# History loads in three pieces, turns in the order of landing, and a uniform step on TensorE

## The reference

```
q = (target_item @ W_q).reshape(b, H, HD)
k = (history_sequence @ W_k).reshape(b, S, H, HD)
v = (history_sequence @ W_v).reshape(b, S, H, HD)
scores = jnp.einsum('bhd,bshd->bhs', q, k) / SCALE
scores = jnp.where(mask[:, None, :] == 0, NEG, scores)
attn = jax.nn.softmax(scores, axis=-1)
out = jnp.einsum('bhs,bshd->bhd', attn, v).reshape(b, A)
return out @ W_o
```

## Time and profile before

| | before |
|---|---|
| median of 3 runs | 578.87 us (578.73 to 581.99) |
| the profiled execution: time, span | 578.07 us, 576.1 us |
| PE, DVE busy | 538.1 us (93%), 504.2 us (88%) |
| ACT, POOL busy | 291.3 us (51%), 309.2 us (54%) |
| HBM | 217.58 MB read, 380 GB/s over the span |
| chain that ended last | PE 71%, DVE 17%, DMA 5%, issue 5% |
| DVE turns (L475) | 320, 472.1 us busy |

### The profile page before, as it was taken

One profiled execution on the slowest core, in us unless ns is written; L12 is line 12 of the kernel. 1 busy time (PEld: TensorE's weight loads), 2 busy tenths in 40 slices (PEclk: granted clock), 3 DMA queues, 4 the chain that ended last, 5 costly groups with the idle time before them and its releaser, 6 DMA issues.

```text
span 576.1 us, 41624 instructions
## 1 busy us (share of the span) xinstructions
PE 538.1 (93%) x18604; PEld 437.8 (76%) x18604; DVE 504.2 (88%) x577; ACT 291.3 (51%) x949; POOL 309.2 (54%) x1126
## 2 busy tenths in 40 slices
PE   5597999999999999999999899999999999999996
PEld 4475878778787877877787787878778787877875
DVE  5657899999999899999998999999999999999970
ACT  2053545554555555455555545545554554555453
POOL 6653456465655556565555556556465645646500
PEclk9799999999999999999999999999999999999999
DMA  8967999999999999999999999999999999999950
GB/s 327 416 259 278 354 406 411 402 405 405 412 404 409 405 406 405 405 413 398 410 406 403 385 395 408 406 403 409 405 405 405 409 402 399 410 407 401 402 213 7
DMA packets 47687, 219.04 MB, mean 380 GB/s; under 512 B 5696, under 2 KB 14416, under 8 KB 47648
## 3 DMA queue, kind: packets, MB, share of 16 engines
q1 hardware_dynamic: 46368, 217.35, 94.8%
q0 software_dynamic: 704, 1.05, 0.5%
q10 hardware_dynamic: 576, 0.25, 0.2%
HBM read 217.58 MB, written 1.05 MB: 380 GB/s over the span
## 4 chain that ended last, share of the span: by engine, by line
PE 71%; DVE 17%; DMA 5%; issue 5%; SPq 1%; ACT 0%; DVEq 0%; POOLq 0%; POOL 0%
PE ps_s L251 27%; PE ps_c L281 23%; DVE blocks L475 15%; PE ps_p L264 7%; PE ps_y L291 6%; PE ps_u L239 3%; PE ps_u L298 3%; DMA x_t<-r_target_item 3%; DMA hist<-r_history_sequence 2%; DVE probs_t L496 1%; SPq L153 1%; PE ps_y L306 1%; ACT p_pad L410 0%; DVE inv_sum L491 0%; SPq L144 0%
## 5 line engine op out<-in xcount | busy, mean ns | idle before, releaser
L475 DVE STREAM_TRANSPOSE blocks<-hist 128x768 f32<-128x768 f32 (+2 forms) x320 | 472.1, 1494 | 25.4 <-DMA hist<-r_history_sequence 23.2
L199 POOL COPY u_pad<-u_sb 32x32 f32<-32x32 f32 x1024 | 236.3, 231 | 111.6 <-ACT u_sb L389 53.7
L251 PE MATMUL ps_s<-blocks,u_pad 128*32 128x200 f32 x4096 | 193.7, 335 | 16.5 <-DVE blocks L475 14.4
L281 PE MATMUL ps_c<-hist,p_pad 64*32 64x128 f32 x12800 | 199.8, 271 | 4.0 <-issue 3.1
L281 PEld LDWEIGHTS ps_c<-hist,p_pad 64*32 64x32 f32 x12800 | 181.8, 105 | 19.8 <-issue 17.3
L410 ACT ACTIVATE p_pad<-ps_p,own 128x200 f32<-128x200 f32 x512 | 170.1, 443 | 42.4 <-PE ps_p L264 42.4
L251 PEld LDWEIGHTS ps_s<-blocks,u_pad 128*32 128x32 f32 x4096 | 122.8, 109 | 72.2 <-issue 26.5
L203 POOL TENSOR_SCALAR bias<-mask 128x200 f32<-128x200 int32 x64 | 56.5, 883 | 128.1 <-DMA mask<-r_mask 127.7
L419 ACT COPY ctx_sb<-ps_c 128x128 f32<-128x128 f32 x128 | 27.8, 269 | 88.5 <-PE ps_c L281 88.5
L393 ACT ACTIVATE probs<-neg_score,neg_max 128x200 f32<-128x200 f32 x64 | 29.4, 459 | 81.2 <-DVE neg_max L484 81.1
L264 PE MATMUL ps_p<-probs_t,place_sel 128*64 128x112 f32 x1024 | 63.7, 267 | 0.8 <-DVE probs_t L496 0.5
(11 more groups left out here) (42 smaller groups left out, 93.0 us busy)
## 6 DMA issues: line engine op xcount, KB each, us to landing
hist<-r_history_sequence SPq DMA_DIRECT2D x128, 832.0 KB, 8.6
hist<-r_history_sequence SPq DMA_DIRECT2D x128, 768.0 KB, 5.9
mask<-r_mask SPq DMA_DIRECT2D x64, 100.0 KB, 8.6
out<-out_sb POOLq DMA_DIRECT2D x21, 48.0 KB, 5.3
x_t<-r_target_item SPq DMA_DIRECT2D x1, 976.0 KB, 16.1
w_in<-L_rec_W_k ACTq DMA_DIRECT2D x1, 64.0 KB, 2.0
w_in<-L_rec_W_q SPq DMA_DIRECT2D x1, 64.0 KB, 2.2
w_in<-L_rec_W_v ACTq DMA_DIRECT2D x1, 64.0 KB, 6.7
```

The lines of the kernel that those rows point to most:

```text
L199: pool.tensor_copy(to, source[Q * c:Q * c + Q, a]).then_inc(u_pad_ready, 1)
L251: mm = pe.matmul(ps_s[ring][Q * b:Q * b + Q, 0:S].rearrange("p (t j) -> p t j", j=J), u_pad[ring][:, i, b, c, :], blocks[slot][:, :, c, J ...
L281: mm = pe.matmul(ps_c[alpha][at:at + Q, 0:D], p_pad[rows, t + par, i, :], hist[2 * ring + i][rows, t + par, :], start=(t == 0), stop=(t + ...
L475: dve.transpose(blocks[g % BLOCKS][:, t0:t1].rearrange("p t c k -> p (t c k)"), hist[g % SLOTS][:, t0:t1, :].rearrange("p t d -> p (t d)") ...
```

## The change

The history of a group is loaded in three pieces of 6, 9 and 10 columns, each with its own semaphore and its own release by the context. DVE turns each piece by itself, six turns a pair, in the order in which they are loaded. PE's step is the same for all three steps of a round: place, turn_context, both scores, context; the projection or the outputs stand between the second and the third piece of the context. The projection of a round is made two rounds ahead, half of the heads in the second step and half in the third; those of rounds 0 and 1 are made before the loop. The target rows of the first two rounds are loaded early on ACT's queue, the rest behind the history of pair 2, and the wait for them moves into the projection. The wait for the expanded weights moves to the last matmul of the scores. ACT copies the projection and the outputs ahead of the context. Cut to its core:

```
-    HALVES = ((0, 12), (12, T))
+    PIECES = ((0, 6), (6, 15), (15, T))
+    SIGNAL = (0, 1, 2)
...
             for p in range(NP):
-                for h, (t0, t1) in enumerate(HALVES):
+                for h, (t0, t1) in enumerate(PIECES):
                     for i in range(2):
                         g = 2 * p + i
-                        wait(sp, ctx_done, 2 * (p - RING) + h + 1)
+                        wait(sp, ctx_done, len(PIECES) * (p - RING) + h + 1)
...
-                if p == 1:
-                    sp.dma_start(x_t[:, ROUND:B], target_t[:, ROUND:B]).then_inc(rest_loaded, 16)
+                if p == 2:
+                    sp.dma_start(x_t[:, 2 * ROUND:B], target_t[:, 2 * ROUND:B]).then_inc(rest_loaded, 16)
...
-            def combine(r):
+            def combine(r, heads):
                 if not isinstance(r, int):
-                    pe.wait_ge(u_copied, r)
+                    pe.wait_ge(rest_loaded, 16)
+                    if heads[0] == 0:
+                        pe.wait_ge(u_copied, r)
                 at = r * ROUND
-                for h in range(H):
+                for h in heads:
...
+                        if released is not None and c == 3 and b == B4 - 1:
+                            pe.wait_ge(expanded, released)
...
                 place(q)
-                if ring < 2:
-                    pe.wait_ge(ctx_copied, 2 * q + 2)
-                    turn_context()
-                    if ring == 0:
-                        combine(r + 1)
-                    if ring == 1:
-                        outputs(q - 1)
-                    scores(q + 1, after, 0)
-                    pe.wait_ge(expanded, q + 1)
-                    scores(q + 1, after, 1)
+                pe.wait_ge(ctx_copied, 2 * q + 2)
+                turn_context()
+                scores(q + 1, after, 0)
+                scores(q + 1, after, 1, q + 1)
+                for piece in range(len(PIECES) - 1):
+                    context(ring, piece)
+                if ring == 0:
+                    outputs(q)
                 else:
-                    scores(q + 1, after, 0)
-                    scores(q + 1, after, 1)
-                    pe.wait_ge(expanded, q + 1)
-                    pe.wait_ge(ctx_copied, 2 * q + 2)
-                    turn_context()
-                context(ring, 0)
-                context(ring, 1)
+                    combine(r + 2, (2 * ring - 2, 2 * ring - 1))
+                context(ring, len(PIECES) - 1)
...
+            pe.wait_ge(u_copied, 1)
+            combine(1, range(H))
             warm(WARM[0])
             scores(0, 0, 0)
             scores(0, 0, 1)
-            pe.wait_ge(rest_loaded, 16)
             warm(WARM[1])
...
-            act.dma_start(x_t[:, 0:ROUND], target_t[:, 0:ROUND]).then_inc(x_loaded, 16)
+            act.dma_start(x_t[:, 0:2 * ROUND], target_t[:, 0:2 * ROUND]).then_inc(x_loaded, 16)
...
                 normalise(q)
+                r = q // RING
+                if q % RING == 0 and r + 1 < NR:
+                    copy_combined(r + 1)
+                if q % RING == 1 and r >= 1:
+                    store(r - 1)
                 if q >= 1:
                     finish(q - 1)
...
                 if p < NP:
-                    turn(p, 1, 0, 0, 6)
+                    turn(p, 1, 0)
                 if p >= 1:
                     reciprocal(p - 1)
                 if p < NP:
-                    turn(p, 1, 0, 6, 12)
+                    turn(p, 0, 1)
                 if p >= 1:
                     turn_probs(p - 1)
                 if p < NP:
-                    turn(p, 0, 1)
                     turn(p, 1, 1)
+                    turn(p, 0, 2)
+                    turn(p, 1, 2)
```

## The result

The changed kernel takes 592.77 us (median of 4 runs, 590.92 to 593.22), the kernel before 580.43 us beside it: a ratio of 1.0225, interval 1.0188 to 1.0262. It is 12 us slower; 581.5 us was forecast, and the range ended at 588.

A forecast was written before the change was run, and what follows sets the result against it. Transfers, PE and DVE were all taken to stand within a few per cent of the step, tied by chains. First maximum +1.0, 63 steps +2.2, tail +0.2: +3.4 us on 578.07 gives 581.5 us, range 577 to 588.

The forecast's parts named there:

- The six turns in the order of landing: DVE, 44 columns behind the maximum for 38: a floor of 8.63 us a step, 0.26 us over 8.37.
- The chain of 8.63 us runs from the first M on: Loop start, M being the maximum's start: target rows in two parts end the slow start, gaining 14.1 us.
- The projection of round 1 before the loop: Ahead of the first warm-up: eight more matmuls delay the first maximum by 1.0 us, bounds 0.8 to 2.0.
- PE's order: PE's step with the projection inside the context: 8.63 us in a round's first step, 8.19 us in the others.
- The wait for the expanded weights: Before the last score matmul: ACT's eight copies, 2.66 us, end before the wait, covered by the scores.
- ACT's order: ACT's projection and output copies ahead of the context's: 0.6 us beside place and turn, hidden.
- The pieces: Six history transfers a pair for four: loss at joints 0.35 us for 0.23, hidden; DMA share under 1.
- the transfers bound it and the early release pays: Rival, 8%: DMA sets the step, 551 us at 8.14 us a step, 565 us with only the start repaired.
- the two equal chains add up: Rival, 20%: in a round's first step PE's and DVE's 8.63 us have no slack between them; together 589 us.

The follow-up runs named there:

- eights: The changed kernel with pieces of 8, 8 and 9 columns instead of 6, 9 and 10: 587.52 us, ratio to the kernel before 1.011.
- split_only: The kernel before with only the turn of 12 columns cut into 6 ahead of the maximum and 6 behind: 599.94 us, ratio 1.0331.
- two_ahead: The changed kernel with both turns of 6 columns ahead of the maximum: 577.91 us, ratio to the kernel before 0.9962.
- start_only: The kernel before with only the target rows of two rounds loaded early, the rest behind pair 2: 577.63 us, ratio 0.9972.
- warm_more: The changed kernel with 28 transposes instead of 16 ahead of the loop: 593.16 us.
- sixes: The changed kernel with both turns of 6 ahead of the maximum, projection and outputs outside the context, pieces 6, 6, 13: 575.86 us.
- peel: The changed kernel with the first round of three steps written out ahead of the loop: 922.82 us, ratio 1.5943.

## Why the prediction missed, point by point

**The six turns in the order of landing: right, with luck in the last 0.04 us.** 8.63 us from maximum to maximum forecast, 8.64 measured in all three steps. The chain that was added up ends with the pair's last turn and the second half of the scores. In the trace the last turn ends at 313.11, and 313.11 + 1.68 would be 8.60 us from maximum to maximum. The scores, though, run as one group of 64 behind one wait, that for the last turn of group 0 (it ends at 311.72, the scores start at 311.85 and take 2.98 us to the maximum: 8.64). In the step with the outputs PE does not wait at all, and its own order of 8.63 us is the limit. The prediction had left out the second way, which eights shows as the longer one; that it came out equal here is chance. split_only shows that the turns alone do it, two_ahead that without them the loss is gone. The slope was read right (1.28 us for a turn of 9). The floor as such is shown.

**"The chain of 8.63 us runs from the first M on": wrong, by 10.2 us.** This is the step that failed. I had taken the slow start of 14.1 us as one thing that goes away with the wait for the target rows. It was three. The wait for the rows put the first place 6 us late (27.24 us, against 21.21 in start_only); that wait did go away, and the place started at 22.33 us where 22 was forecast. PE's pauses for its code, 5.2 us, stood in the same stretch and stayed (6.35 us after). So did a stretch at half the clock. Before, it made the 16 transposes take 3.65 us and the first place 1.53, after 1.97 and 0.99; after, it cost 1.7 us in the first step (warm_more) and 1.5 us behind the longest pause (1.10 for 0.61 and 2.30 for 1.30). Pauses and half clock are together 9.5 of the 10.1 us that four steps lose against steady ones. start_only measures the term by itself: the first four steps get 4.7 us shorter, the fifth maximum comes 4.0 us earlier and the medians differ by 2 us, where 13 were counted on. With the 46.7 us of before kept for these four steps, the prediction's sum gives a span of 591.7 us; 591.3 were measured. The rows that showed it lay in front of me: the chain of the kernel before lists the pauses as "issue" at 35, 45 and 51 us, and I had read only the waits that had a name.

**The projection of round 1 before the loop: right in kind, 1.5 us for 1.0.** The warm-up started 1.82 us behind it, PE had begun 0.68 us later (11.34 us against 10.66), and the shorter warm-up (3.25 us against 4.29) gave 1.04 back.

**PE's order: right.** The step with the outputs was read as 8.63 us and measured as 8.65 in two_ahead, where nothing else covers it. The Trainium skill ("TensorEngine Tiling (Array Packing)", Key Properties) has the array drain when the tiling mode changes; the trace agrees: entering and leaving the context for a projection takes 0.20 us from start to start each time, where context matmuls follow each other every 0.016 us on the average and those of the projection after 0.11.

**The wait for the expanded weights, ACT's order: no sign of either.** The scores with that wait inside take 2.91 us in the steady part, as long as those ahead of the loop, which have none. ACT's order shows nowhere either: the steps are 8.64 us, and PE's only idle time is the 0.36 and 0.22 us before the scores in two steps of three (none in the third), where 0.4 was forecast.

**The pieces: right that they cost nothing here, wrong in what would show it.** I had written that the DMA share would fall under 1. It is 1.02 at 397 GB/s, as at 406 before, although landings were waited for only 4 times. The rule on large transfers in the Trainium skill ("DMA: Bandwidth & Descriptors", Bandwidth) did not bite: six transfers a pair of 384 to 640 KB run as fast as the step asks, and up to 407 GB/s in sixes, with six of 384 to 832 KB. The 2.0 us fixed per transfer that the prediction sets beside this rule is a fit of the same page of the Trainium skill (Anatomy of one DMA) for transfers that GpSimd issues; these are issued by SP, and no run here measures a fixed part.

**The rivals.** That the transfers bound it and the early release pays: not so. That the two equal chains add up: not so either, the steady step is within 0.02 us of the floor. The miss came from a term that no rival put in doubt.

## What to carry to other kernels

Write down, for every in-order engine, what stands between its input from a partner and the output that the partner waits for; that sum is a floor for the step, and moving an instruction from the free side of the hand-over to the bound side lengthens that sum by its full time, and each step by what was not slack (0.88 us and 0.35 us in split_only). Cutting work into finer pieces moves such borders without anyone intending it; look at which side each piece falls on. When a slow start is to be credited to a change, account for each microsecond of it by name first, the unnamed pauses too: here PE loaded its code in the first pass of the loop, and that stayed.

## What the runs showed of the hardware that was not expected

- PE's loop of three steps has some 112 KB of code in seven pieces of 16 KB. In the first pass of the loop the pauses for it were 0.3 to 3.8 us long (the kernels before and after and start_only); in peel the longest was 7.2 us, and the 178 further pieces cost 1.85 us each. The loop's code stays loaded (9 pieces in the whole run) or is loaded again in each pass (187 pieces, 1.6 times the time), with nothing changed but a round written out ahead of the loop.
- The DMA share does not tell a bound: it stood at 1.02 with 397 GB/s and slack, and at 1.03 with 407 GB/s and DVE waiting for landings (sixes).
- DVE's transpose follows its size closely: 0.88, 1.28 and 1.78 us from start to start for 768, 1152 and 1664 values a partition.
